# A decoder layer on one core: VectorE mixes a tile of the attention one iteration later, directly behind a row maximum

## The reference

```python
x = x + attn(layernorm(x), ...)        # bilinear and trilinear running sums over time, no softmax
x = x + xattn(layernorm(x), ctx, ...)  # below
x = x + ffn(layernorm(x), ...)         # silu(gate) * up, down; all operands quantized to 4-bit blocks of 16

# xattn, per batch entry; S = 1024 tokens, 77 context rows
normed = rmsnorm(hidden) * norm_w
v_pool = concat([normed, memory])
logits = (normed @ q_w.T) @ (v_pool @ k_w.T).T / 16      # causal over tokens, all context rows seen
h_tilde = softmax(logits) @ v_pool
alpha = sigmoid(hidden @ gate_w.T + gate_b)
out = (1 - alpha) * hidden + alpha * h_tilde
```

## Time and profile before

| | |
|---|---|
| three runs | 571.42, 571.68, 571.88 us |
| the profiled execution | 574.74 us, span 572.9 us |
| TensorE busy | 543.2 us (95%) |
| VectorE busy | 456.9 us (80%) |
| GpSimd, ScalarE busy | 344.8 us (60%), 329.9 us (58%) |
| mean granted TensorE clock | 0.985 of full speed |
| share of TensorE in the chain that ended last | 77% |

### The profile page before, as it was taken

How to read it: one execution, slowest core, us unless ns; L and a number is a source line. 1 busy time by engine, 2 the same in 40 slices (tenths; PEclk the granted TensorE clock), 3 DMA queues, 4 the chain that set the end, 5 groups by cost and what they waited for, 6 DMA issues and landing times.

```text
span 572.9 us, 10819 instructions
## 1 busy us (share of the span) xinstructions
PE 543.2 (95%) x3156; PEld 477.2 (83%) x3156; DVE 456.9 (80%) x1163; ACT 329.9 (58%) x742; POOL 344.8 (60%) x470
## 2 busy tenths in 40 slices
PE   4997999999999999999999888999999999999986
PEld 4876888888888888888888766899999999999976
DVE  3587679767798757977578567999999999999984
ACT  4335652737446375462653656777777777777651
POOL 4024928449276384582679527777777777777640
PEclk9998999999999999999999998999999999999998
DMA  8620400000000000000000000000000000000001
GB/s 233 187 76 8 146 2 0 2 2 0 0 0 0 0 1 1 2 1 1 1 1 1 1 1 1 10 19 18 18 18 18 18 19 26 18 18 18 20 19 37
DMA packets 16124, 13.78 MB, mean 24 GB/s; under 512 B 3883, under 2 KB 15839, under 8 KB 16095
## 3 DMA queue, kind: packets, MB, share of 16 engines
q1 hardware_dynamic: 16095, 13.43, 7.7%
HBM read 9.23 MB, written 4.19 MB: 23 GB/s over the span
## 4 chain that ended last, share of the span: by engine, by line
PE 77%; DVE 5%; issue 4%; ACT 4%; POOL 2%; DVEq 0%; ACTq 0%; POOLq 0%
PE ps L892 17%; PE ps L894 17%; PE ps L893 17%; PE ps L1090 9%; PE ps L1233 4%; PE ps L1078 2%; PE ps L1010 2%; PE ps L1011 2%; PE ps L1088 2%; PE ps L1126 1%; PE ps L982 1%; ACT xn_sums L631 1%; DVE nT_l L1308 1%; PE ps L1019 1%; PE ps L1076 1%
## 5 line engine op out<-in xcount | busy, mean ns | idle before, releaser
L892 PE MATMUL ps<-keys_h,nT_h 128*128 128x256 f32 (+6 forms) x304 | 95.1, 313 | 1.9 <-DVE keys_l L1308 1.5
L893 PE MATMUL ps<-keys_l,nT_h 128*128 128x256 f32 (+6 forms) x304 | 92.5, 304 | 0.0
L894 PE MATMUL ps<-keys_h,nT_l 128*128 128x256 f32 (+6 forms) x304 | 92.3, 304 | 0.0
L892 PE MATMUL ps<-parts,xq_parts 128*128 128x512 f32 (+1 forms) x192 | 78.8, 411 | 4.3 <-DVE xq_parts L1491 4.2
L894 PE MATMUL ps<-parts,xq_parts 128*128 128x512 f32 (+1 forms) x192 | 73.4, 382 | 0.0
L893 PE MATMUL ps<-parts,xq_parts 128*128 128x512 f32 (+1 forms) x192 | 72.6, 378 | 0.0
L1090 PE MATMUL ps<-V,probT 128*128 128x256 f32 x288 | 68.5, 383 | 0.0
L674 ACT ACTIVATE prob<-ps,nbias 128x205 f32<-128x205 f32 (+7 forms) x32 | 25.7, 804 | 70.9 <-DVE nbias L1388 70.9
L892 PEld LDWEIGHTS ps<-keys_h,nT_h 128*128 128x128 f32 x304 | 57.8, 190 | 6.1 <-issue 1.9
L1090 PEld LDWEIGHTS ps<-V,probT 128*128 128x128 f32 x288 | 55.4, 193 | 8.1
L893 PEld LDWEIGHTS ps<-keys_l,nT_h 128*128 128x128 f32 x304 | 57.7, 190 | 3.4
(11 more groups left out here) (217 smaller groups left out, 1537.6 us busy)
## 6 DMA issues: line engine op xcount, KB each, us to landing
X<-in_x_dram SPq DMA_DIRECT2D x8, 512.0 KB, 5.3
out_dram<-X SPq DMA_DIRECT2D x32, 128.0 KB, 1.7
early<-in_L_ffn_w_down_dram SPq DMA_DIRECT2D x1, 704.0 KB, 7.0
early<-in_L_ffn_w_gate_dram SPq DMA_DIRECT2D x1, 640.0 KB, 4.4
early<-in_L_ffn_w_up_dram SPq DMA_DIRECT2D x1, 640.0 KB, 5.6
ctx_rows<-in_ctx_dram SPq DMA_DIRECT2D x1, 308.0 KB
early<-in_L_attn_Winv_dram SPq DMA_DIRECT2D x1, 256.0 KB, 3.9
early<-in_L_attn_WQ_dram SPq DMA_DIRECT2D x1, 256.0 KB, 5.1
```

The source lines that it names most:

```text
L892: mm(o, wh, mh, start=start, stop=False, **kw)
L893: mm(o, wh, ml, start=False, stop=False, **kw)
L894: return mm(o, wl, mh, start=False, stop=stop, **kw)
```

## The change

Before, `mix_tile(b, i - 2)` stood near the end of iteration i. Now `mix_tile(b, i - 3)` stands directly behind `max_tile(b, i)`. The last iteration holds two, tile 6 at its front and tile 7 at the old place. The other engines' streams are unchanged.

```diff
                 for i in range(TPB + 2):
                     if 1 <= i < TPB:
                         max_tile(b, i)
+                    if i >= 3:
+                        mix_tile(b, i - 3)
                     if more:
...
-                    if i >= 2:
+                    if i == TPB + 1:
                         mix_tile(b, i - 2)
```

## The result

| | before | after |
|---|---|---|
| median of the runs (range; number) | 571.61 us (571.42 to 571.88; 4) | 586.96 us (585.73 to 587.25; 4) |
| profiled execution, its span | 574.74, 572.9 us | 586.91, 585.1 us |
| TensorE busy | 543.2 us | 543.4 us |
| mean granted TensorE clock | 0.985 | 0.988 |

The changed kernel is slower: the ratio is 1.0244, with a 95% interval from 1.0208 to 1.0279. TensorE has the same 3156 matmuls and is busy for the same time. What was added to the span is time in which it stands still: 29.7 us before, 41.7 now. The clock did not fall more often in all, for its mean rose.

The account below looks back on a forecast made before the run. TensorE was taken as the bound, busy 276.8 of 283.0 us in the four batches. Terms 3.4 + 0 + 6.75 + 3.0 - 0.1 = 13.05 on 571.68 gave 584.7 us, range 579.0 to 590.0 for 8 in 10.

Parts of the forecast that it names:

- Iteration 3: Batches 0 to 2, product of tile 1: TensorE waits 1.1 us each for the moved mix, 3.4 us in all.
- Iterations 4 to 7: Batches 0 to 2: other work stands between logits and product, so no wait, 0; `tri` still ends before `y_half` takes it.
- Batch ends: Iterations 8 and 9: tile 6's signal comes behind `keys_low`, so the product of tile 7 starts 2.25 us later; three times, 6.75.
- The clock: Behind the three batch ends: the granted clock falls to 1.2 GHz twice, 1.5 us each, 3.0 us.
- Batch 3: New waits in iterations 3, 5, 6, 7 cost 4.2 us; 1.7, 1.5 and 1.1 come back: -0.1, between -2.5 and +3.
- The sum: Whole kernel: 3.4 + 0 + 6.75 + 3.0 - 0.1 = 13.05 us slower.
- the base: Runs without the profiler lie 3.06 us below the profiled 574.74, at 571.68; from there the forecast is 584.7.
- collisions of the additions with GpSimd: Rival: moved additions in iterations 5 and 7 take 1.4 us more, adding 4.8 over three batches: 589.5 us; chance 9%.
- The faster case: Rival: earlier maxima end waits if TensorE reaches each product later than the signal: 567.4 us, at best 564.0; chance 5%.
- The sign of being wrong: No wait of line 1088 at the batch ends, or TensorE's idle time in the four batches growing under 7 us.

Follow-up runs that it names:

- e2: The changed kernel with the mix of tile 6 alone put back to its old place: 577.29 us, ratio 1.0074 to the kernel before.
- e3: The kernel before with the mix of tile 6 alone moved to the front of iteration 9, behind keys_low: 585.18 us, ratio 1.0203.
- e9: The changed kernel with four unread filler matmuls before the product of tile 7 in batches 0 to 2: 583.68 us, ratio 1.0201 to the kernel before.
- e4: The changed kernel with the mix of tile i-3 directly ahead of the maximum of tile i, not behind: 590.27 us, ratio 1.0296 to the kernel before.
- e10: The changed kernel run again without edit, beside the kernel before, with a second profile: 586.58 us against 573.11, ratio 1.0239.
- e1: The kernel before run again without edit, with a second profile: 572.92 us, ratio 0.9996.
- e5: The changed kernel with nine unread filler matmuls before the product of tile 7 in batches 0 to 2: 586.99 us, ratio 1.0239 to the kernel before.
- e6: The kernel before with mixes of tiles 0 to 5 in batches 0 to 2 moved to the next iteration, ahead of the maximum: 574.73 us, ratio 1.0027.

## Why the prediction was right

It was right in sign and in mechanism, and near in size: 584.7 forecast, 586.96 measured. Its sum came out near in part by luck, as said below.

- **Iteration 3** (1.1 x 3 = 3.4). The recorded waits are 1.08, 1.08 and 1.00, but the forecast was from start to start, and so measured the product is 1.24, 1.24 and 1.17 later behind its mask. A tenth more goes in the first matmuls behind each wait, 4.0 in all. Most of the excess is the step from VectorE's end to TensorE's start, taken as 0.06 and here 70.67 - 70.53 = 0.14. e2, which keeps these waits and those of batch 3 and drops the batch ends, is 3.8 above its base. Right, 0.6 too low.
- **Iterations 4 to 7** (0). No wait of line 1088 there in batches 0 to 2. `tri` ended at 113.56 against a forecast of 112.65 on the clock of the profile before; the whole stage there is 0.93 later (the first keys product 122.53 against 121.60), so it was where I put it, and `y_half` did not wait for it. Right.
- **Batch ends** (2.25 x 3 = 6.75). From start to start 2.23 for the first, and 0.1 more in the matmuls behind it: 6.9 in all. e3 shows that tile 6 alone brings them. Right.
- **The clock** (2 falls x 1.5 = 3.0). Two falls came, of 1.69 each: 3.4. Their cost is shown by e9. The choice of two was a choice under uncertainty, and e3 and e4, with the same waits, had three: that it was two is luck. The price of one was 0.2 too low.
- **Batch 3** (-0.1). From the mask of iteration 3 to the product of iteration 7 it lost 4.35 (forecast 4.2). Inside, the sizes were off: iteration 6 did not wait (0.7 forecast), and the product of iteration 7 came 1.76 later (1.2 forecast) because of `x_chain(0)`, which I had not put in front of the maximum. Then 2.1 came back at the turn of tile 7 (forecast 1.7), 1.5 for the fall, and 0.8 at the FFN's start (forecast 1.1): 0.0 in sum. But the fall is in only one of the two profiles of the kernel before. In the other pair batch 3 costs 1.6. Right in the first pair; without the fall, 1.7 too low.
- **The sum** (13.05). Batches 0 to 2 cost 14.0 us (13.70 + 0.34), where the terms for them give 13.15. The spans differ by only 12.2 in the first pair and 13.5 in the second, because of the 1.5 us that the kernel before lost near its end, for which the forecast had no term. So the sum is near both by errors of opposite sign. Between medians beside each other (e10) it is 13.5.

What was off most is the base. I carried the sum to the median of 571.68, since the three unprofiled runs lay 3 us below the profiled one, and took this for an effect of the profiler. e1 and the later sets show that the kernel before has two clusters and that its larger sets have medians of 573.1 to 573.8. The changed kernel stayed within 584.4 to 587.3. From 573.5 the same sum gives 586.6. So 1.8 of the 2.3 us between forecast and result stand in the step that went from the profiled execution to the runs; the rest is in the terms above, which cancel.

The rivals: collisions of the additions with GpSimd did occur (the longest instance of line 1402 grew from 2022 to 2604 ns), but no wait of TensorE grew by them in the views above, and `tri` was on time. The faster case failed at the point that was named for it: the signal stayed behind the product in every place where I had worked it out. The sign of being wrong did not come: TensorE's idle time in the four batches grew by 11.0 us, from 6.2 to 17.3, and 7 was the limit.

Still open: why the middle batch end kept its clock in both executions of the changed kernel but not in e3 and e4; why the equal wait near the end is followed by a fall in some kernels only; and which falls make the two clusters (last section).

## What to carry to other kernels

When a consumer is moved behind something on its engine, look for what is waited for by that something: here the mix went behind the second piece of `keys_low`, which waits for ScalarE, which waits for TensorE, so TensorE came to wait for its own products by way of two engines. Three such places cost more than all the other 25 moved mixes (e3 against e2). On a saturated engine, work out a new wait from the end of its input to its own next start, then add what the clock does behind it; and take the base from enough runs to know whether it has one level or two. Before a sum is called right, compare the same instruction in both traces at several places: here a fall that went at the far end hid part of what the change cost.

## What the runs showed of the hardware

**The clock follows a wait loosely.** Waits of 2.0 to 2.1 us between saturated stretches were followed by a stretch at 1.2 GHz at 10 of the 12 batch ends that were profiled with them (two of three in both traces of the changed kernel, all three in e3 and in e4), and 0.65 + 1.68 us were followed by one in one execution of the kernel before and not in the next. With the same delay but less idle time (e9) none followed. The wait of 2.3 us near the end of the FFN is in all twelve traces, and a fall follows it in six (both of the kernel before, e3, e4, e5, e6). The Trainium skill, TensorE: Matmul & The Clock Gate (What's actually happening, table of the two states), lists the cold clock as what follows an idle stretch; these runs agree in direction, but a wait of the same length did both.

**A fall is free where TensorE waits anyway.** The fall at 343.9 us of the kernel before cost nothing (the shift was 13.69 before and behind it); one behind a batch end cost 1.69, and the one near the end 1.5.

**The two clusters go with the clock.** Every run has its mean granted clock on record, profiled or not. The 69 later runs of the kernel before are 30 of 571.0 to 572.1 us, all with 0.988 to 0.994, and 39 of 572.8 to 575.5, of which 37 have 0.985 and two 0.988. So the slower cluster spent more time at the lower clock. Where, only a profile tells, and both profiled executions (574.74, 573.61) are of the slower one. Three falls are known to come and go with a price: that in batch 3 (1.5 us), that near the end (1.5 us), and one at the change from preparation to the batches, which the kernel before, the changed kernel and others have and the profiled execution of e9 has not. The stretch in the kernel before, then in e9:

```profile
53.50:56.80 3.30, 2.75 (x13) 2.75 (x14) 2.16 (x12) 1.56 (x6) 2.99 (x9) 0.53 0.09 12
```

```profile
53.50:56.80 3.30, 3.30 (x28) 3.14 (x27) 2.33 (x7) 2.49 (x7) 3.14 (x8) 1.00 0.33 99
```

In e9 the first transposes of the batches start at 63.54 us, against 66.11 in the changed kernel: 2.6 us earlier. That execution took 580.93 us at a mean clock of 0.997; four of the other five took 583.4 to 583.7 at 0.994. Which of these falls parts the clusters of the kernel before is not shown.

**An fp32 matmul can be two passes.** In e5 nine calls with fp32 operands gave 18 records, about 0.22 us from one to the next with 256 columns (3.89 us for 18).
